# Moving the first three up-projection weight loads ahead of two clears and two small loads

## The reference

```python
x = layernorm(x + attn(x, w_qkv, b_qkv, w_out, b_out))     # x: 4 x 2048 tokens x 2048
# attn: one head as wide as the model; softmax(q k^T / sqrt(2048)) v, then w_out
w_up   = ((w_up_q   - 7.5) * repeat(w_up_scale,   64, axis=1)).T    # 2048 x 8192
y1 = x  @ w_up   + b_up   + x  @ w_up_lora_a   @ w_up_lora_b
x2 = relu(y1)
w_down = ((w_down_q - 7.5) * repeat(w_down_scale, 64, axis=1)).T    # 8192 x 2048
y2 = x2 @ w_down + b_down + x2 @ w_down_lora_a @ w_down_lora_b
x = layernorm(x + y2)
```

## Time and profile before

| what | us |
|---|---|
| two timed runs | 3066.49 and 3158.69, median 3112.59 |
| the profiled execution, its own time | 2978.46 |
| its span on the slowest core (core 4) | 2976.9 |
| spans of the 8 cores | 2905.2 to 2976.9 |
| stage C on core 4, first up matmul to the last down matmul | 1403.7 to about 2850 |

### The profile page before, as it was taken

The page is one execution under the profiler, slowest core; times in us unless marked ns, Lnnn a source line. Parts: engine busy times, 40 slices in busy tenths (PEclk is TensorE's granted clock), DMA queues, the critical chain, the costliest instruction groups (busy, mean ns, idle before and its releaser), DMA issues.

```text
span 2976.9 us, 31824 instructions; the slowest of 8 cores (2905.2 to 2976.9 us)
## 1 busy us (share of the span) xinstructions
PE 2113.4 (71%) x11704; PEld 1022.2 (34%) x11856; DVE 669.3 (22%) x719; ACT 433.1 (15%) x886; POOL 440.5 (15%) x469
## 2 busy tenths in 40 slices
PE   0899987888677774762767688565876777767861
PEld 0344457777333231320323233222332223223310
DVE  0000000000110124014124242322413224142356
ACT  0112122122221241133100001010000100001031
POOL 2000000000000001001223132222322223231300
PEclk9999999899888886885979899887997889988955
DMA  9653323322416414764999999999999999999902
GB/s 134 95 88 43 43 38 55 54 42 42 88 44 130 74 36 143 133 92 47 84 94 111 93 104 98 97 89 77 101 95 90 87 90 100 95 96 78 86 10 109
DMA packets 729859, 246.13 MB, mean 83 GB/s; under 512 B 597520, under 2 KB 716352, under 8 KB 729696
## 3 DMA queue, kind: packets, MB, share of 16 engines
q0 software_dynamic: 627184, 189.54, 66.0%
q1 hardware_dynamic: 102528, 54.55, 6.8%
HBM read 404.10 MB, written 25.17 MB: 144 GB/s over the span
## 4 chain that ended last, share of the span: by engine, by line
PE 44%; DMA 36%; DVE 6%; issue 6%; ACT 4%; another core or an unknown queue 3%; POOL 2%; DVEq 0%; ACTq 0%; SPq 0%; POOLq 0%
DMA s_ds<-sexpd 12%; PE pp L376 11%; DMA s_us<-sexpu 11%; PE pp L824 9%; PE pp L873 8%; DMA v_scr<-s_qev 7%; PE pp L506 4%; PE pp L591 3%; PE pp L639 3%; DMA s_wo<-woutT 3%; PE pp L411 2%; DVE s_uq L755 1%; POOL s_dq L167 1%; ACT s_qev L421 1%
## 5 line engine op out<-in xcount | busy, mean ns | idle before, releaser
L873 PE MATMUL pp<-s_x,s_dq 128*128 128x512 bf16 x2006 | 490.8, 402 | 230.8 <-DVE s_acc L882 204.8
L824 PE MATMUL pp<-s_xlnb,s_uq 128*128 128x512 bf16 x2005 | 500.6, 403 | 203.4 <-DVE s_uq L755 193.4
L376 PE MATMUL pp<-s_xbf,s_wq 128*128 128x512 bf16 x1506 | 332.7, 381 | 84.2 <-DMA s_wq<-wqkvT 82.6
L873 PEld LDWEIGHTS pp<-s_x,s_dq 128*128 128x128 bf16 x2048 | 204.5, 102 | 516.9 <-issue 317.4
L824 PEld LDWEIGHTS pp<-s_xlnb,s_uq 128*128 128x128 bf16 x2048 | 207.4, 103 | 484.3 <-issue 277.2
L411 PE MATMUL pp<-s_wq,s_xbf 128*128 128x128 bf16 x4096 | 262.6, 227 | 70.1 <-ACT s_qev L421 69.6
L411 PEld LDWEIGHTS pp<-s_wq,s_xbf 128*128 128x128 bf16 x4096 | 248.6, 102 | 84.2 <-issue 78.5
L837 ACT ACTIVATE s_x<-pp,s_bu 128x512 bf16<-128x512 f32 x128 | 87.9, 687 | 1284.8 <-PE pp L831 1254.6
L755 DVE SCALAR_TENSOR_TENSOR s_uq<-s_uq,s_us 128x2048 bf16<-128x2048 bf16 x64 | 146.0, 2290 | 517.1 <-DMA s_us<-sexpu 517.1
L785 DVE SCALAR_TENSOR_TENSOR s_dq<-s_dq,s_ds 128x1024 bf16<-128x1024 bf16 x128 | 156.8, 1225 | 429.2 <-DMA s_ds<-sexpd 429.2
L376 PEld LDWEIGHTS pp<-s_xbf,s_wq 128*128 128x128 bf16 x1536 | 150.9, 98 | 265.5 <-issue 85.9
(11 more groups left out here) (83 smaller groups left out, 972.3 us busy)
## 6 DMA issues: line engine op xcount, KB each, us to landing
s_uq<-wupqT POOLq DMA_DIRECT2D x64, 512.0 KB, 15.2
s_us<-sexpu POOLq DMA_DIRECT2D x64, 512.0 KB, 21.3
s_dq<-wdnqT POOLq DMA_DIRECT2D x128, 256.0 KB, 5.9
s_ds<-sexpd POOLq DMA_DIRECT2D x128, 256.0 KB, 6.7
s_wq<-wqkvT POOLq DMA_DIRECT2D x24, 1024.0 KB, 10.0
s_wo<-woutT POOLq DMA_DIRECT2D x16, 1024.0 KB, 13.5
s_vp<-v_scr SPq DMA_DIRECT2D x16, 1024.0 KB, 6.3
s_xbf<-xT POOLq DMA_DIRECT2D x16, 512.0 KB, 34.1
```

The source lines that it names most:

```text
L376: e.matmul(pp[bank][:, 0:tn], buf[:, dc * PA + oc * 128: dc * PA + oc * 128 + 128], s_xbf[:, dc * T + t0: dc * T + t0 + tn], start=(dc == ...
L824: e.matmul(pp[bank][:, 0:tn], uq_v[u % NBUF][:, dc, :], s_xlnb[:, dc * TO + t0: dc * TO + t0 + tn], start=(dc == 0), stop=False)),
L873: e.matmul(pp[bank][:, 0:tn], dq_v[key % NBUF][:, i, :], s_x2[:, i * TO + t0: i * TO + t0 + tn], start=(i == 0), stop=(i == GS - 1))),
```

## The change

The loop that issues the first three `load_up` is moved up, ahead of the two clears and the two small loads. Its waits stay as they are (`pe_wo_end` and `dve_h1_end`), and so do all other lines.

```diff
@@ -789,6 +789,9 @@
               inc=dve)
             dn_dve[key] = dve.n
 
+        for u0 in range(min(NBUF, GS * NG)):
+            load_up(u0)
+
         E("a", lambda e: e.memzero(s_bupl[:, :]),
           waits=[(pe, endB["pe"]), (act, endB["act"]), (dve, endB["dve"]),
                  (po, endB["po"])], inc=act)
@@ -799,8 +802,6 @@
         DMA("g", dlb, s_bdnl[0:R, :], bdnl[:, :])
         dlb_all = dlb.n
 
-        for u0 in range(min(NBUF, GS * NG)):
-            load_up(u0)
 
         for gi in range(NG):
             for i in range(GS):
```

## The result

The changed kernel took 2974.37 us, the median of 35 executions (2930.55 to 3110.46); the kernel before took 2996.84 us, the median of 34 (2951.19 to 3158.69). The ratio is 0.9927, with a 95% interval of 0.9897 to 0.9958: about 22 us less, 13 to 31. Of the two timed executions that the prediction had (median 3112.59), one was the longest of the 34 and the other the seventh longest; the profiled one, at 2978.46, was much nearer to the median.

The account below looks back on a forecast made before the run. Stage C was taken to wait for its weight transfers, DMA being at nine tenths or more. From the median 3112.59 us, 18.5 us of saved DVE idle time (small loads' cost 0) gave 3094 us, range 2960 to 3140.

Parts of the forecast that it names:

- The mechanism: Start of stage C: six up transfers run during the idle norm, so the first dequantisation starts at 1382.5 rather than 1401.03.
- 37 us of slack: Six early transfers: landed by about 1345, while nothing asks for them before 1382.4.
- The term of 18.5 us: First dequantisation on core 4: 18.60 us of DVE idle time, less about 0.1 us between two instructions, is gained.
- the base of the sum: Kernel time before, 3112.59 us, the median of the timed runs, from which 18.5 us was subtracted.
- the reading of its size: Whole kernel: 2%, 62 us, taken as what a measurement can tell from no change; 0.82 to within 2%.
- likeliest range of 11.3 to 24.5: Gain in the likeliest case, 3088 to 3101 us: from core 5's possible loss to core 4's fourth-tile stall gone.
- Rival 1: End of stage B: neighbour's last output-projection load is slowed, core 5 keeps 11.3 us of gain; 3101 us, chance 0.12.
- Rival 2: Stage C, fourth tile: core 4 no longer stalls 5.97 us there, gain 24.5 us; 3088 us, chance 0.12.
- Rival 3: Stage C: the earlier start is given back as the pair's loads fall against each other; 3113 us, chance 0.08.
- Rival 4: Stage C: the two cores of a pair fall into a worse rhythm, costing 35 us; 3129 us, chance 0.13.
- The balance of bytes: Stage C: a pair's first six tiles, 31.3 us of transfers, leave the busy stretch, which begins 14.5 later: 16.8 us.
- the chain's 18.5: Stage C through PE: tile, free buffer, load and dequantisation all move 18.5 us earlier, the fourth load to 1404.0.

## Why the prediction came out as it did

**The mechanism was right for the first tile.** Six transfers in the idle stretch of the norm, no wait at the first dequantisation, everything else where it was, the fourth load earlier by the same amount: the timeline after shows each of these steps. One term of it was off without harm: the six transfers were put at 18 us, from the 174 GB/s of a 15 us stretch, and took 28 on core 4; 31 of the 37 us of slack were left.

**The size of the shift was a little low.** The term of 18.5 us was read from the slowest core. The mean over the cores was more: on three of the eight, each some 11 us behind its neighbour, the first matmul had come at 88 to 89 us instead of 81 to 83. The neighbour's first loads, still running, are the likely reason (core 5, 19 us behind its neighbour, came at 82.8), argued and not tried by itself. The first matmul moved by 21.5 us (85.1 to 63.6). At group 1, 19.2 us were kept. The ratio says about 22 us, the pairs' ends say 13 +-3; the 18.5 forecast lies between, and no measure here is sharper than that.

**Two steps failed, the base of the sum and the reading of its size.** They are the next two paragraphs; the step from the trace to the shift held.

**The chances were wrong.** The ratio is within 2%, where 0.82 of the chance lay, but its interval excludes 1, and what I put down as not to be told from no change is a real gain of 0.73%. I knew the gain as 18.5 us with a likeliest range of 11.3 to 24.5, all of one sign, and then blurred it with 2% as the limit of what can be told. Some 35 executions a side gave an interval of +-0.3%.

**The level was wrong.** The term 3112.59 us of the sum, the median of two executions, is 2996.84 over 34: 116 us too high, more than five times the gain. So 3094 us lies above even the kernel before, and the changed kernel's median is 2974. That the range held it is luck: its lower end was built from the profiled execution (2960), 14 us below. With three numbers at hand I should have given the profiled one more weight: it fell near the later median of 34. Why executions of one kernel differ by so much stays open.

**Rival 1** (the neighbour's load) exists, if it is the cause there, at 3.5 us on one core of 32. **Rival 2** (tile 3's stall) came true on core 4 and not on its pair: core 4 reaches tile 3 24.3 us earlier (120.1 to 95.8 from the end of stage B), but core 5 after stalls there for 6.55. In all 16 pairs of the changed kernel the fourth load is in 9.9 to 10.8 us after its issue on the core that runs ahead and 14.4 to 18.6 on the other; before, it was 13.1 to 18.8 on all. So the mean gain at tile 3, 22.8 us, is only 1.3 above that at tile 0. **Rival 3** is refuted up to group 2; at group 4 three traces of four show the gain. **Rival 4**, the rhythm, is no effect of the change: it differs as much between two traces of the same kernel, and spreads the pairs' ends of both kernels by about 35 us (one standard deviation).

**The balance of bytes was a wrong account with a right number.** It gave 16.8 us beside the chain's 18.5, and I took that as support. The partial moves show that bytes as such don't count: two thirds of them alone gave 1.7 us, and one third less of them cost nothing. What counts is when PE finishes tile 0, and that tiles 1 and 2 are in by about then; with both late, 8.8 us were lost.

Open is how much of the shift reaches the end: 16 +-10 us by the traces, 13 +-3 by the pairs' ends, 13 to 31 by the ratio.

## What to carry to other kernels

Where a stage is fed by a stream of loads that is gated by buffers, find the instruction that frees the first buffer; a load moved earlier is worth what it brings that instruction forward, and the bytes moved are worth something only as far as they would not have been in by then. Look at what else stands in the list of the engine behind an early wait: here a dequantisation waiting for its load held up two small copies in one variant and a layer norm in another. And when executions scatter by 35 us, measure at a checkpoint near the edit, where 20 us stand out after one trace.

## What was new of the hardware

Replacing a 128-row matmul by one of 16 rows between 128-row ones did not save time but cost 0.21 us each: 3.88 us against 3.67 from one to the next, in all three kernels with 16 rows against all those with 128. Of the two cores of a pair, here 10 to 28 us apart and mostly some 11, the one ahead had 1 MB (two 512 KB loads, weights and scales) in 9.9 to 10.8 us and the one behind in 14.4 to 18.6, in all 16 pairs of the changed kernel (fourth load of each core).
